# Attention over a graph: loads moved between two queues, heads handled in pairs, and the edge parts placed by a fused compare-and-multiply

## What is computed

```python
logits = jnp.einsum('ehd,ehd->eh', q[src], k[dst])
a = logits + dist_attn + path_attn          # per edge and head
e = jnp.exp(a - segment_max(a, dst)[dst])
sa = e / segment_sum(e, dst)[dst]
agg = segment_sum(v[src] * sa[:, :, None], dst)
x = agg @ Wo + bo
```

## Time and profile before

| | |
|---|---|
| time, 3 runs | 818.81 us median (812.48 to 819.82) |
| profiled execution | 812.19 us, span 810.2 us |
| VectorE busy | 532.6 us, 66% |
| TensorE busy (matmul) | 696.5 us, 86%, mean granted clock 0.944 |
| ScalarE busy | 417.8 us, 52% |
| Pool busy | 121.8 us, 15% |
| DMA | 125.6 MB, mean 155 GB/s |

### The profile page before, as it was taken

The page is one execution under the profiler, slowest core; times in us unless marked ns, Lnnn a source line. Parts: engine busy times, 40 slices in busy tenths (PEclk is TensorE's granted clock), DMA queues, the critical chain, the costliest instruction groups (busy, mean ns, idle before and its releaser), DMA issues. The chain is left out here.

```text
span 810.2 us, 14580 instructions
## 1 busy us (share of the span) xinstructions
PE 696.5 (86%) x4978; PEld 547.9 (68%) x4978; DVE 532.6 (66%) x1162; ACT 417.8 (52%) x689; POOL 121.8 (15%) x187
## 2 busy tenths in 40 slices
PE   3988755787879765999999999999999999999994
PEld 2654333454546442599999679968889899887793
DVE  6737594897989531644322654358878888888855
ACT  5235332675767651754333643237767666676640
POOL 7341264242420021000000001300000000000022
PEclk9999886898989976999999999999999999999997
DMA  9734395657565764300002040966767677766114
GB/s 250 193 60 92 77 140 140 201 151 215 170 195 188 235 182 145 128 1 1 1 1 79 0 156 26 377 202 218 247 206 226 235 237 241 259 224 230 64 58 152
DMA packets 104156, 125.62 MB, mean 155 GB/s; under 512 B 32402, under 2 KB 70060, under 8 KB 103564
## 3 DMA queue, kind: packets, MB, share of 16 engines
q1 hardware_dynamic: 96955, 115.06, 45.8%
q0 software_dynamic: 5600, 6.54, 3.5%
q10 hardware_dynamic: 1520, 3.01, 1.8%
HBM read 94.91 MB, written 29.67 MB: 154 GB/s over the span
## 5 line engine op out<-in xcount | busy, mean ns | idle before, releaser
L2220 PE MATMUL ps<-xT,w_hi 128*128 128x480 f32 (+7 forms) x512 | 110.5, 338 | 2.2 <-DVE hT L2039 2.2
L2220 PEld LDWEIGHTS ps<-xT,w_hi 128*128 128x128 f32 x512 | 82.1, 189 | 9.4 <-DVE hT L2039 4.0
L2025 DVE TENSOR_TENSOR w_lo<-weights_far,w_hi 128x1024 fp32r<-128x1024 f32 x64 | 78.0, 1219 | 2.5 <-ACT w_hi L2135 2.2
L2222 PEld LDWEIGHTS ps<-xT,w_lo 128*128 128x128 f32 x512 | 73.5, 190 | 1.5
L2222 PE MATMUL ps<-xT,w_lo 128*128 128x240 f32 (+7 forms) x512 | 74.5, 268 | 0.0
L193 POOL DMA_DIRECT2D windows<-window_scratch x104 | 59.7, 577 | 93.0 <-DVE onehot L990 76.2
L1113 PE MATMUL ps<-onehot,group_weights 128*32 128x314 bf16 x1272 | 59.7, 331 | 15.8 <-DVE onehot L990 8.2
L2135 ACT ACTIVATE w_hi<-weights_far 128x1024 fp32r<-128x1024 f32 x64 | 67.1, 1051 | 0.0
L990 DVE TENSOR_SCALAR onehot<-iota_h,windows 128x628 bf16<-128x628 f16 x212 | 66.8, 378 | 0.0
L2245 PE MATMUL ps<-w_hi,hidden 128*128 128x512 f32 (+3 forms) x176 | 62.2, 405 | 2.7 <-DVE hidden L2049 1.9
L1135 PE MATMUL ps<-ident,weights 126*128 126x126 f32 (+1 forms) x200 | 34.0, 308 | 32.2 <-ACT weights L1072 22.6
(11 more groups left out here) (309 smaller groups left out, 1530.4 us busy)
## 6 DMA issues: line engine op xcount, KB each, us to landing
weights_far<-in_L_ffn_w SPq DMA_DIRECT2D x64, 512.0 KB, 5.6
sums_scratch<-sums_out SPq DMA_DIRECT2D x53, 314.0 KB, 3.3
weights_near<-in_L_ffn_w SPq DMA_DIRECT2D x32, 512.0 KB, 3.5
sums_in<-sums_scratch SPq DMA_DIRECT2D x40, 309.1 KB
weights_near<-in_L_gnn_W SPq DMA_DIRECT2D x4, 1024.0 KB, 13.3
weights_near<-in_L_ffn_sw SPq DMA_DIRECT2D x8, 512.0 KB, 5.0
weights_near<-in_L_gnn_Wqkv SPq DMA_DIRECT2D x3, 1024.0 KB, 8.2
weights_ff<-in_L_gnn_W SPq DMA_DIRECT2D x1, 3072.0 KB, 13.0
```

The lines of the kernel that those rows point to most:

```text
L2025: dve.tensor_tensor(to[1], raw_rest[n] if v == V else raw[u][n], to[0], ALU.subtract)\
L2220: pe.matmul(both(bank, cap), w[u % 2][0][:, c, cut], xT(r)[:, c, :, :], start=c == 0, stop=False)
L2222: last = pe.matmul(bank[:, 0:cap], w[u % 2][1][:, c, cut], xT(r)[:, c, 0, :], start=False, stop=c == DC - 1)
```

## The change

- **Compare and multiply.** `mask` and its product go. For each of a block's four groups one `scalar_tensor_tensor` compares the constant `nodes` (72 numbers) with the window's node number and multiplies with the parts (72 numbers). The constant is made once by Pool.
- **Pairs.** One maximum over both units of a pair (1,256 numbers, two results) replaces two; one reciprocal of two totals replaces two. One row load of 618 KB into one of two buffers replaces two of 309 KB.
- **Loads.** Pool loads only blocks with `w % 4 == 3`, SyncE the other three of four. SyncE's `load_starts` reads three blocks (12 values) at a time, Pool's one block (4 values). Five blocks are considered ahead of the stage, of which SyncE loads 0, 1, 2 and 4; Pool loads block 3 inside the attention. SyncE loads block `w + 6` ahead of the store of block `w`, and blocks up to 17 ahead of pair 0's rows.
- **Stores.** The 14 leading blocks are stored from ScalarE's queue, each right behind its copy.
- **Collect** moves from VectorE to ScalarE, in front of the two norms.
- **Bias loads** move from SyncE's end to ScalarE's start of the attention.

```diff
-LOADED = 6
+LOADED = 5
+POOLS = 3
...
 def by_pool(w):
-    return w % 4 >= 2
+    return w % (POOLS + 1) == POOLS
...
-            for w in range(window_blocks(0) + 1):
-                block(w)
-            unit_rows(0)
-            unit_rows(1)
-            for w in range(window_blocks(0) + 1, leading):
-                block(w)
+            for w in range(LOADED, window_blocks(0) + 7):
+                load(w)
+            pair_rows(0)
+            for w in range(window_blocks(0) + 7, leading + AHEAD):
+                load(w)
             for q in range(PAIRS):
                 if q + 1 < PAIRS:
-                    unit_rows(2 * q + 2)
-                    unit_rows(2 * q + 3)
+                    pair_rows(q + 1)
                 for w in pair_blocks(q):
-                    block(w)
+                    load(w + AHEAD)
+                    stored(w)
...
+            def load(w):
+                nonlocal starts, first
+                if w < WB and not by_pool(w):
+                    if w % (POOLS + 1) == 0 or starts is None:
+                        starts, first = load_starts(nc, mybir.EngineType.SP, w, POOLS - w % (POOLS + 1), tab), w
+                    wait_past(sp, windows_stored, stored_for(w))
+                    window_free(sp, w)
+                    load_groups(sp, w, starts[(w - first) * GW:], rec2_d, windows, g_in)
+            def stored(w):
+                sp.wait_ge(w_copied, w + 1)
+                sp.dma_start(sums_d[w, :, :], sums_out[w % 3]).then_inc(out_done[w % 3], 16)
...
-                dve.tensor_tensor(mask[w % 2], windows[:, w % RING, :, 0:1].broadcast_to([P, GW, GD]),
-                                  offsets[:, k0 * GD:(k0 + GW) * GD].rearrange("p (j d) -> p j d", d=GD), ALU.is_equal)\
-                   .then_inc(masked, 1)
-                dve.tensor_tensor(R[w % 3][:, :, 0:GD * H, :].rearrange("p j (d h) a -> p j d (h a)", h=H),
-                                  parts[:, w % RING, :, 4:4 + 3 * H].unsqueeze(2).broadcast_to([P, GW, GD, 3 * H]),
-                                  mask[w % 2].unsqueeze(3).broadcast_to([P, GW, GD, 3 * H]), ALU.mult).then_inc(r_ready, 1)
+                for j in range(GW):
+                    last = dve.scalar_tensor_tensor(
+                        out=R[w % 3][:, j, 0:GD * H, :].rearrange("p (d h) a -> p d (h a)", h=H), in0=nodes[:, (GW * w + j) % GPB],
+                        scalar=windows[:, w % RING, j, 0:1],
+                        in1=parts[:, w % RING, j, 4:4 + 3 * H].unsqueeze(1).broadcast_to([P, GD, 3 * H]), op0=ALU.is_equal, op1=ALU.mult)
+                last.then_inc(r_ready, 1)
...
+            def guards(q):
+                dve.wait_ge(s_ready, q + 1)
+                wait_past(dve, e_ready, 2 * q)
+                dve.tensor_reduce(small[0:TILE, 1:3], both[0:TILE], AX.XY, ALU.max, negate=True).then_inc(g_ready, 1)
+            def inverses(q):
+                dve.wait_ge(summed, 2 * q + 2)
+                dve.reciprocal(small[0:TILE, 5:7], small[0:TILE, 3:5]).then_inc(inv_ready, 1)
...
                 act.activation(halves(sums_out[w % 3]), psW(w), ACT.Copy).then_inc(w_copied, 1)
+                if w < leading:
+                    act.wait_ge(w_copied, w + 1)
+                    act.dma_start(sums_d[w, :, :], sums_out[w % 3]).then_inc(out_done[w % 3], 16)
...
             for q in range(PAIRS):
                 ws = list(pair_blocks(q))
+                if q:
+                    collect(q - 1)
                 norm(2 * q)
                 norm(2 * q + 1)
```

More of the change, by code:

```diff
@@ L168, in by_pool, with load_starts @@
 def by_pool(w):
-    return w % 4 >= 2
[L173 to L181, removed]
+    return w % (POOLS + 1) == POOLS
+def load_starts(nc, engine, w, blocks, tab):
+    n = min(blocks * GW, GROUPS - GW * w)
     _, starts = nc.values_load_multi_w_load_instructions(tab[0:1, REL + GW * w:REL + GW * w + n], engines=[engine], min_val=0,
@@ L448, in _ @@
                 if not by_pool(w):
[L449 to L450 removed]
+                    if w % (POOLS + 1) == 0:
+                        starts = load_starts(nc, mybir.EngineType.SP, w, min(POOLS, LOADED - w), tab)
+                    load_groups(sp, w, starts[w % (POOLS + 1) * GW:], rec2_d, windows, g_in)
             sp.dma_start(wo[:, :, :], Wo.rearrange("(c p) n -> p c n", p=P)).then_inc(wo_in, 16)
@@ L486, in _ @@
                                parts[:, b0:b0 + nb, :, 5:5 + 3 * H - 1:3], ALU.subtract).then_inc(lo_ready, 1)
[L487 to L492, removed]
         @block.vector
@@ L839, in attention @@
         sums_out = [sb(f"sums_out{i}", [P, SRC]) for i in range(3)]
-        sums_in = [sb(f"sums_in{i}", [P, SRC]) for i in range(4)]
+        sums_in = [sb(f"sums_in{i}", [P, 2 * SRC]) for i in range(2)]
         L = [sb(f"exponents{i}", [P, SRC]) for i in range(2)]
@@ L866, in attention_units @@
     out_done = [sem(f"sums_out{i}") for i in range(3)]
-    units_in = [sem(f"units_in{i}") for i in range(4)]
+    units_in = [sem(f"units_in{i}") for i in range(2)]
     def halves(tile):
@@ L889, in _, with pair_rows @@
         with sp.If(longest < CHUNK + 1):
[L890 to L899, removed]
+            starts, first = None, None
+            def load(w):
[7 more added lines that the diff above has]
+            def stored(w):
                 sp.wait_ge(w_copied, w + 1)
                 sp.dma_start(sums_d[w, :, :], sums_out[w % 3]).then_inc(out_done[w % 3], 16)
-            def unit_rows(u):
-                tile, h = divmod(u, H)
+            def pair_rows(q):
+                tile, h = divmod(2 * q, H)
                 if h == 0:
@@ L942, in _ @@
             exact = dict(allow_small_or_imprecise_dtypes=True)
[L943 to L945 removed]
+            pool.iota(nodes.rearrange("p k d c -> p (k d) c"), [[1, GPB * GD], [0, 3 * H]], base=0, channel_multiplier=0, **exact)\
+                .then_inc(consts, 1)
             for i in range(3):
                 pool.memset(R[i][:, :, GD * H:DH // 2, :], 0.0).then_inc(consts, 1)
[L948 to L957 removed]
+            pool.wait_ge(consts, 5)
+            for w in range(POOLS, WB, POOLS + 1):
+                starts = load_starts(nc, mybir.EngineType.Pool, w, 1, tab)
+                wait_past(pool, windows_stored, stored_for(w))
+                window_free(pool, w)
+                load_groups(pool, w, starts, rec2_d, windows, g_in)
         pool.wait_ge(ff_vec_in, 80)
@@ L1098, in _ @@
                     copied(w)
+            collect(PAIRS - 1)
     @block.tensor
```

104 lines of the change are left out of this document (31 added, 73 removed).

## The result

The changed kernel takes 831.25 us in the median of 4 runs (829.87 to 834.61), the kernel before on the same chip 819.32: ratio 1.0168, 95% interval 1.0101 to 1.0234. By the medians it is slower by 12 us, by the means, which the ratio takes, by 14. The forecast was 828, with 814 to 840 as its range and 0.62 on slower by over 1%. The profiled execution is the slowest of the four: 834.61, span 833.0, 22.8 us above the profiled one of before, which is among the fastest of its kernel (812.19 beside 812.48 to 821.06).

The account below looks back on a forecast made before the run. Two coupled near-equal bounds were named, VectorE at 23.7 and SyncE at about 23 us per three pairs. Lead-in, loop and end terms summed to +12.1 us, 824 on the profiled execution, 831 on the median; 828 was named, range 814 to 840.

Parts of the forecast that it names:

- SyncE's queue as the place of the loss: Attention loop: SyncE's in-order loads, stores and register batches grow from 23.0 to 26.2 us per three pairs.
- Compare-and-multiply: VectorE, each block: four scalar_tensor_tensor at 0.29 us replace mask and product, a block 2.03 us instead of 1.66.
- The rival of the small terms: Batch stays at 3.3 us, scalar_tensor_tensor 0.145 apart: +1 to +5 us, 815 to 821; chance 0.27.
- The loop: Attention pairs, S(0) to S(12) (first `weights` of pairs 0, 12): 29.0 us per three pairs against 26.4, +10.5 us.
- both high: Rival: batch 5.0, landing 6.3, three pairs 31 us, S(0) +7; +23 us, 839 to 842; chance 0.13.
- Lead-in: Before pair 0's first `weights`: SyncE issues pair 0's rows at 137.0 against 133.93, start 3.9 us later.
- From S(12) to pair 16, and the transfers of the last pairs: Pair 12's first `weights` to pair 16's row issue: -0.2 us; pairs 16 to 19, led by transfers, unchanged.
- The end: Attention's end: last pair's tail 0.45 us longer, Pool's five additions no longer last, -2.6 us.
- The additions are hidden in Pool's idle time: With the biases loaded early, Pool's five additions cost nothing at the attention's end: -2.6 us.
- The sum: Whole kernel: 3.9 + 10.5 - 0.2 + 0.45 - 2.6 = +12.1 us.
- VectorE alone counts: Rival: `sums_in` waits vanish, batches of 12 cost 2 us, three pairs 26.0; -6 to -8 us; chance 0.10.

Follow-up runs that it names:

- e1_split: Changed kernel with SyncE loading two of four blocks in batches of 8 values and Pool the other two: 812.63 us, ratio 0.9979 to the kernel before.
- e3_fixed: Changed kernel with SyncE reading no start values in the attention, each window loaded from a fixed place: 804.73 us, ratio 0.9848 to the kernel before.
- e2_mask: Changed kernel with the old mask and single product in place of the four scalar_tensor_tensor: 831.63 us, ratio 1.0212 to the kernel before.
- e7_order3: Changed kernel with SyncE issuing all of a pair's window loads in front of its stores: 829.64 us, ratio 1.0192 to the kernel before.
- e8_late: Changed kernel with Pool's five additions held until pair 15's totals are there: 829.82 us, ratio 1.019 to the kernel before.
- e4_bias: Kernel before with only the five bias loads moved from SyncE's end to ScalarE's start of the attention: 808.9 us, ratio 0.9927.

## Why the prediction was right, point by point

The direction, the cause and the median were right. That the median lies within 4 us of the forecast is in part luck: the loop cost twice what I had for it, the end gave back almost four times what I had, and the two errors partly offset each other. Between the two profiled executions, on which the sum was built, I had 12.1 us and it was 22.8.

**SyncE's queue as the place of the loss: right, shown.** Undoing the split alone takes back 15 us by the ratios (e1_split); taking the reads out of the queue takes back 26 (e3_fixed); undoing the VectorE part takes back nothing (e2_mask). The chain store, batch, loads, store, loads, store, rows, landing is in the timeline as written.

**Compare-and-multiply: right.** 305 ns each (0.29 said), 1.99 us per block (2.03 said), maximum of the pair 1.46 (1.46 said). VectorE's busy time per three pairs grew by 1.8 us (2.1 said). The rival of the small terms had 0.145 apart; it is 0.205.

**The loop: right in kind, mis-sized.** I had 29.0 us per three pairs and +10.5 in twelve pairs; it was 32.0 and +22.5 between the two profiled executions. The copy that starts the chain came as said, 5.2 us after S(1) for 5.0. Four terms were low. The batch of 12 registers leaves gaps of 4.4 to 5.5 us, mean 4.9, where I took 4.3. The 0.25 us for each value were right; the fixed part was not, because the TENSOR_LOAD in front of them took 1.2 to 2.15 us in the loop, where it had taken 1.0 to 1.5 in the kernel before. The row load of 618 KB lands in 5.6 to 6.1 us, where I took 5.2 (5.3 in the lead-in). A group of four loads took 2.1 us on average, not 1.9. And up to 0.3 us stand before each further group of loads and 0.05 before a store or row load, 1.5 us per three pairs, which my sum of issues left out. From 162 to 258 us SyncE's work adds up to 30.3 us per three pairs of 32.1, not 26.2: the queue was nearly full, so nearly everything in it counted, not one chain per pattern. This was the rival "both high", to which I gave 0.13; in the loop it is what happened (31 us said), while the median stands at the forecast, because the end gave back more than I had counted.

**Lead-in: right in kind, mis-sized.** +3.9 said, +8.2 in this execution, +5.2 in e7_order3 and e8_late, whose lead-in is the same. Pair 0's rows went out at 141.30, not 137.0. This was not the batches, whose gaps were 4.1 to 4.3 us as said, but the ten groups of loads: they took 22.9 us without what stands between them, where I had 19. ScalarE's 14 stores did end its waits there and were not what came last. Unforeseen but covered: VectorE waited 5.1 us for block 3's windows, now loaded by Pool inside the attention.

**From S(12) to pair 16, and the transfers of the last pairs: right within the scatter.** -0.2 said for all of it, -1.5 measured up to S(19): +0.9 to S(16), and -2.3 from there, which I had unchanged.

**The end: right in kind, mis-sized on both sides.** -2.15 said for the tail and the additions together, -8.0 measured. From S(19) to the last copy it is 1.7 us more where I had 0.45; from there to the next stage 9.7 us less where I had 2.6. Before, 8.2 us passed between Pool's last addition and the next stage; after, 1.1 us between ScalarE's last copy and the next stage. I had counted only Pool's lead over VectorE and left out Pool's DRAIN, as if what follows on Pool would follow anything. "The additions are hidden in Pool's idle time" failed as well: Pool was idle, VectorE was not, and one pair grew by 4.6 us in e4_bias and by about 5 in e3_fixed (14.1 us, where others with three blocks take 9.0). In the changed kernel even that is hidden behind SyncE (e8_late).

**The sum.** Between the profiled executions: +8.2 lead-in, +22.5 loop, -1.5 to S(19), -8.0 end, +1.5 in the later stages, 22.8 in all where I had 12.1. Between the medians it is 12. Which of the terms is smaller in the other executions isn't settled: only one of each is in a trace. The lead-in of e8_late is 3 us shorter than the changed kernel's with nothing changed there, so single profiled terms vary by that much.

**The rival "VectorE alone counts": excluded.** It needed a batch under 2.3 us. e3_fixed is what it would have looked like: 26.0 us per three pairs and a ratio of 0.985, faster than before.

## What to carry to other kernels

Add up each issuing queue as one adds up an engine: loads, stores, register reads and the waits between them, per pattern. When the sum comes near the pattern's length, as 30.3 of 32.1 here, work saved elsewhere brings nothing: neither VectorE's shorter block (e2_mask) nor the hold-up taken away (e8_late) was worth anything measurable here. Then ask of each entry whether it stands behind something that it doesn't need. Giving each queue one kind of work (loads on SyncE, stores on the engine that makes the data) and issuing what is ready a step early, together with half of the loads back on Pool and the old mask and product, turned a change that lost 12 us into one that gains 22. The ratios of the steps: 1.0168 changed, 0.9979 loads divided as before, 0.9895 loads ahead of stores, 0.9898 old mask, 0.9789 rows a pair earlier, 0.971 stores from ScalarE. Where an edit ends a wait at a stage's end, look at what follows the last instruction there: it can be worth more than the instruction.

## What was unexpected of the hardware

Reading values from an on-chip table into a sequencer's registers is dear: on SyncE the gap was about 1.9 us for 2 values, 3.3 to 4.2 for 8 in the kernel before, and 4.4 to 5.5 for 12 in the changed one. Of it 0.25 us goes to each value; the rest is one TENSOR_LOAD, 0.75 to 1.0 us for 12 values in the lead-in and 1.2 to 2.15 in the loop. Five additions of 128x512 f32 on Pool stretched VectorE's four one-hots from 1.25 to 8.11 us, and in the changed kernel a reduction from PSUM in the same stretch kept its 1.46. One load of 618 KB was there after 5.3 to 6.1 us where the first of two with 309 KB took 4.4 and the second 6.3. And the next stage started 8.2 us after Pool's last addition but 1.1 us after ScalarE's last copy. Pool's DRAIN at the end of the stage ended 7.9 us after its last addition in all eight kernels in which Pool loads half of the blocks, and 4.3 us after it in all six in which Pool loads a quarter. So it goes with Pool's share of the loads; that this is the cause wasn't tried by itself.
